# Where the bulk loads are begun, how a step of probabilities is transposed, and four orders of instructions, in a layer of local and global attention with a final linear part

## The chip, the cores and the metric

The kernel runs on one core of a Trainium2 chip. Its time is the device time of one launch in microseconds (us). TensorE (PE) multiplies matrices, VectorE (DVE) and ScalarE (ACT) work on elements, GpSimd (POOL) does casts and begins some transfers, SyncE (SP) begins transfers only. The profile reads one execution of the program.

## The reference

The input is x of shape (4, 1024, 1024): 4 batches, 1024 tokens, 1024 channels, 16 heads of 64. Everything is float32.

```
h  = layernorm(x);  q, k, v = h@Wq+bq, h@Wk+bk, h@Wv+bv        # split into 16 heads of 64
local:  each block of 128 queries attends to 256 keys, [i*128-64, (i+1)*128+64), masked at both ends
idx:    token 0, the 62 tokens of the largest |q| of the head, token 1023
global: softmax(q[idx] k^T / 8) v over all 1024 keys, written over the rows idx of the local result
x = x + ctx
out = x + layernorm(x) @ (w * scale[:, None])^T + bias
```

## The kernel before

A program for each engine is written out by hand. Engines meet at counting semaphores. Every matmul of a projection is done three times: a float32 operand is split into a high part (`_hi`) and the remainder (`_lo`), and hi*hi, hi*lo and lo*hi are added up.

**A batch** has a query part (8 slices of 128 query columns are projected, q is turned, norms are taken, and VectorE begins to find the 62 largest norms, 8 at a time: MAX, FIND_INDEX, MATCH_REPLACE, L1450 to L1454), and then 8 **units**, hp = 0 to 7. A unit is a pair of heads. It has four local steps, s = 0 to 3 (two query blocks of 128 for both heads in each), and a global step, called STEPS in the code. After the four batches come 32 tiles of the final linear part (L799); two of them are done ahead, inside the last unit.

**TensorE in a unit** works in this order: scores 0 (L745), part 0, weigh step 3 of the unit before (L757), part 1, scores 1, global weigh of the unit before (L779), part 2, scores 2, part 3, weigh 0, part 4, scores 3, part 5, weigh 1, part 6, global scores (L771), weigh 2, part 7. A part is 12 of the 96 matmuls (L639) that project the keys and values of the next pair. Parts 0 to 3 make v (two halves of the tokens), 4 to 7 make k. In unit 6 the order is v half 0 (parts 0, 1), k half 0 (2, 3), v half 1 (4, 5), k half 1 (6, 7), and part 6 comes after weigh 2. The halves go through PSUM banks that ScalarE empties: `out("v", 1, 2)` (vT, L1075) empties the bank of v half 1 before k half 1 (part 6) may write there.

**A step of probabilities** takes this way: VectorE takes the row maxima (L1510, L1513); ScalarE takes the exponentials (L1105); VectorE copies them as two planes of 16-bit words, `part_p` (`p_parts<-probs`, L1496); SP begins a transposing DMA, `turn_p` (`p_turned<-p_parts`, L295); ScalarE puts the planes together again, `join_p` (`pT<-p_turned`, L1127); TensorE weighs the values with the result (L757, L779). Each of the copy, the DMA and the join is done in two halves of 1024 words (the last of the global step has 1280). There is one `p_parts` and one `p_turned`. So the DMA of a half waits for the join of the same half of the step before. The values go the same way in three pieces of 768 words (`part_v` L1486, `turn_v` L305, `join_v` L1092).

**SP's order.** All of this program's transfers but the gathers, scatters and the last stores are begun by SP, one behind the other; an instruction of SP that waits for a semaphore holds all behind it. SP begins in each unit, besides the transposing DMAs and the context stores: two loads of 512 KB of the weights' slices (`w_raw`, L387 at the unit's start, L412 in its middle), one of 512 KB with columns of the next batch's x (`load_column`, L322), and in units 0 and 1 two of 512 KB with rows of x (`load_rows`, L314) for the row statistics. POOL splits each slice into its parts (`split`, L500 and L502).

**Row statistics of the next batch** are taken by VectorE (BN_STATS, L1322) in the query part (tile pair 0) and in units 0 to 2 (pairs 1 to 3). `row_roots` follows in unit 3, then SP writes the statistics to DRAM (`save_stats`, L337) at that unit's end and reads them back spread over the partitions (`spread_stats`, L347) at the start of unit 4, ahead of the transposing DMA of step 0. VectorE's normalising of the columns (L1392, L1395) needs them from unit 4 on. In the last batch `spread_scale` and `load_ahead` stand in that place instead, and `load_first` (L372, L373) starts four loads for the final linear part in the last unit.

## Time and profile before

| | before |
|---|---|
| median of 3 runs | 2244.83 us (2239.55 to 2246.85) |
| the profiled execution | 2241.47 us |
| its span | 2239.5 us |
| its mean TensorE clock | 0.95 of full speed |
| TensorE busy | 2039.9 us, 91% |
| units 0 to 6 of the four batches, together | 1237.63 us |

The span is the time from the first to the last instruction of the profile. A unit's length is taken from one unit's first matmul of scores 0 to the next one's.

### The profile page before, as it was taken

How to read it: one execution, taken by the hardware profiler on the slowest of the kernel's cores; microseconds unless marked ns; L12 is line 12 of the kernel's file. 1: busy time of each engine (PE TensorE's matmuls, PEld its weight loads, DVE VectorE, ACT ScalarE, POOL GpSimd, SP SyncE). 2: the span in 40 equal slices, each digit the busy share in tenths (PEclk: the TensorE clock that was granted, in tenths of full speed). 3: DMA queues.
4: the chain of work that ended last, by engine and by line, in shares of the span. 5: the costliest groups of instructions: out<-in, count | busy, mean ns of one | idle time of the engine just before them, and what ended most of it. 6: DMA issues, size and time to landing. Idle time of an engine off the chain costs nothing.

```text
span 2239.5 us, 37450 instructions
## 1 busy us (share of the span) xinstructions
PE 2039.9 (91%) x11264; PEld 1698.9 (76%) x11264; DVE 1524.9 (68%) x2904; ACT 1047.0 (47%) x1979; POOL 523.3 (23%) x336
## 2 busy tenths in 40 slices
PE   6989797999988879999888699998998997999999
PEld 6877685787867767888677578886887876888887
DVE  6687675774876757748777577577785775666664
ACT  4325555683256646742465466624675682000000
POOL 2241121123321121132321312233222202212221
PEclk9999898999989989999999899999999998999999
DMA  4346656654365566643465556524666645333331
GB/s 154 91 103 132 143 123 117 137 121 130 88 146 129 134 114 124 132 130 113 110 135 138 118 132 132 123 83 97 138 142 169 153 78 166 141 131 127 136 140 66
DMA packets 539680, 280.73 MB, mean 125 GB/s; under 512 B 439120, under 2 KB 504726, under 8 KB 539536
## 3 DMA queue, kind: packets, MB, share of 16 engines
q1 hardware_dynamic: 531888, 261.21, 49.0%
q10 hardware_dynamic: 4320, 15.73, 1.7%
q0 software_dynamic: 3328, 2.17, 0.5%
q8 instruction: 54, 0.88, 0.2%
q14 instruction: 90, 0.74, 0.1%
HBM read 122.73 MB, written 51.44 MB: 78 GB/s over the span
## 4 chain that ended last, share of the span: by engine, by line
PE 47%; DVE 18%; DMA 11%; ACT 9%; issue 8%; SPq 6%; DVEq 1%; ACTq 0%; POOL 0%; POOLq 0%
PE proj L639 20%; PE proj L799 15%; DMA p_turned<-p_parts 7%; PE pv L757 4%; ACT pT L1127 4%; SPq L295 3%; DVE x_norm L1454 3%; ACT probs L1105 3%; DVE top_val L1450 2%; DVE p_parts L1496 2%; DVE top_idx L1452 2%; PE score L771 2%; DVE q_sq L1416 2%; DMA stat_rows<-ln_rstd 1%; PE pv L779 1%
## 5 line engine op out<-in xcount | busy, mean ns | idle before, releaser
L639 PE MATMUL proj<-xT_hi,w_hi 128*128 128x512 f32 x1536 | 447.2, 438 | 99.5 <-ACT vT L1075 79.9
L639 PEld LDWEIGHTS proj<-xT_hi,w_hi 128*128 128x128 f32 x1536 | 302.5, 207 | 169.3 <-ACT vT L1075 83.2
L639 PE MATMUL proj<-xT_hi,w_lo 128*128 128x512 f32 x1536 | 425.8, 407 | 0.0
L500 POOL CAST w_hi<-w_raw 128x1024 fp32r<-128x1024 f32 x96 | 114.2, 1189 | 1225.4 <-PE proj L639 1147.6
L639 PE MATMUL proj<-xT_lo,w_hi 128*128 128x512 f32 x1536 | 381.9, 391 | 0.0
L1127 ACT COPY pT<-p_turned 128x1024 uint16<-128x1024 uint16 x256 | 344.0, 1362 | 71.5 <-DMA p_turned<-p_parts 71.5
L639 PEld LDWEIGHTS proj<-xT_hi,w_lo 128*128 128x128 f32 x1536 | 291.6, 196 | 62.9
L639 PEld LDWEIGHTS proj<-xT_lo,w_hi 128*128 128x128 f32 x1536 | 288.5, 188 | 63.7
L1496 DVE COPY p_parts<-probs 128x1024 uint16<-128x1024 uint16 x320 | 259.4, 820 | 113.7 <-ACT probs L1105 58.1
L757 PEld LDWEIGHTS pv<-v_nat,pT 128*128 128x128 f32 x2048 | 261.5, 201 | 78.1 <-issue 68.2
L757 PE MATMUL pv<-v_nat,pT 128*128 128x64 f32 x2048 | 257.2, 281 | 64.8 <-ACT v_nat L1092 64.8
L502 POOL TENSOR_TENSOR w_lo<-w_raw,w_hi 128x1024 fp32r<-128x1024 f32 x96 | 238.7, 2487 | 7.8
L1105 ACT ACTIVATE probs<-turn,neg_max 128x256 f32<-128x256 f32 (+1 forms) x256 | 115.3, 457 | 184.4 <-DVE neg_max L1510 127.0
L1105 ACT ACTIVATE probs<-score,neg_max 128x256 f32<-128x256 f32 (+1 forms) x256 | 116.1, 465 | 95.1 <-DVE neg_max L1513 83.3
L559 POOL TENSOR_TENSOR q_store<-q_store,bias_b 128x1024 f32<-128x1024 f32 x30 | 71.8, 2392 | 332.0 <-DVE q_store L1791 251.8
L1416 DVE TENSOR_TENSOR q_sq<-pT 128x512 f32<-128x512 f32 x64 | 71.8, 1121 | 111.0 <-ACT pT L1049 109.8
L1082 ACT ACTIVATE kT_hi<-proj,bk_c 128x512 fp32r<-128x512 f32 x64 | 44.0, 688 | 181.5 <-PE score L771 143.2
L1519 DVE TENSOR_REDUCE neg_max<-score 128x1 f32<-128x1024 f32 x32 | 39.1, 1223 | 104.3 <-PE score L771 104.3
L1127 ACT COPY pT_g<-p_turned 128x1024 uint16<-128x1024 uint16 x64 | 96.0, 1502 | 15.3 <-DMA p_turned<-p_parts 14.6
L1040 ACT ACTIVATE pT<-proj,bq_c 128x512 f32<-128x512 f32 x48 | 33.1, 689 | 140.8 <-PE proj L639 140.8
L1092 ACT COPY v_nat<-v_turned 128x768 uint16<-128x768 uint16 x96 | 98.4, 1082 | 0.0
L1132 ACT CAST qT_hi<-turn 128x1024 fp32r<-128x1024 f32 x15 | 15.2, 1016 | 159.9 <-PE turn L788 159.9
(169 smaller groups left out, 3068.9 us busy)
## 6 DMA issues: line engine op xcount, KB each, us to landing
w_raw<-in_wstream SPq DMA_DIRECT2D x96, 512.0 KB, 3.8
x_buf<-in_rows SPq DMA_DIRECT2D x55, 512.0 KB, 3.4
q_rows<-pT SPq DMA_DIRECT2D x64, 256.0 KB, 2.4
ctx_rows<-ctx_out SPq DMA_DIRECT2D x128, 128.0 KB, 2.1
q_store<-ctx_rows SPq DMA_DIRECT2D x30, 512.0 KB, 4.1
out<-q_store ACTq DMA_DIRECT2D x30, 512.0 KB, 2.6
q_store<-in_cols SPq DMA_DIRECT2D x28, 512.0 KB, 3.6
p_turned<-p_parts SPq DMA_TRANSPOSE x320, 3.3
```

Source lines behind the costliest of these rows:

```text
L295: sp.dma_start_transpose(p_turned[:, 2 * words.start:2 * words.stop].rearrange("p (x r) -> p x r", r=P), p_parts[:, 2 * words.start:2 * wo ...
L500: pool.tensor_copy(w_hi[b][:, :], w_raw[b][:, :]).then_inc(w_hi_set, 1)
L502: pool.tensor_tensor(w_lo[b][:, :], w_raw[b][:, :], w_hi[b][:, :].bitcast(F32), ALU.subtract).then_inc(w_split[b], 1)
L559: pool.tensor_tensor(lin_hb[:, b, :], lin_h[:, b, :], bias_b[:, :], ALU.add).then_inc(hb_set, 1)
L639: mm = pe.matmul(proj[:, bank, :], w[b][:, k * P:k * P + P], x[:, k, half * HALF:half * HALF + HALF], start=(m == 0), stop=(m == 23), skip ...
L757: mm = pe.matmul(pv[:, g * HD:g * HD + HD], pT_of(s)[:, (g * 2 + c) * P:(g * 2 + c) * P + P], v_nat[:, 2 * s + b + c, h, :], start=(c == 0 ...
L799: mm = pe.matmul(proj[:, half, :], x[b][:, k * P:k * P + P], w[:, k, half * 512:half * 512 + 512], start=(m == 0), stop=(m == 23), skip_gr ...
L1092: act.copy(v_nat[:, 3 * k:3 * k + 3, :, :].rearrange("p t h d -> p (t h d)").bitcast(U16) .rearrange("p (x s) -> p s x", s=2), v_turned[:, ...
L1105: last = act.activation(probs[:, at:at + hi - lo], score_of[s][:, at:at + hi - lo], ACT.Exp, bias=neg_max[:, g:g + 1], accum_out=row_sum[: ...
L1127: act.copy(pT_of(s)[:, words].bitcast(U16).rearrange("p (x s) -> p s x", s=2), p_turned[:, 2 * words.start:2 * words.stop].rearrange("p (s ...
L1416: dve.tensor_tensor(q_sq[:, :], src, src, ALU.mult).then_inc(q_squared[h], 1)
L1496: dve.tensor_copy(p_parts[:, 2 * words.start:2 * words.stop].rearrange("p (s x) -> p s x", s=2), probs[:, words].bitcast(U16).rearrange("p ...
```

## The change

(a) The loads of `w_raw`, of the columns, of row pair 3 and of `load_first` are begun by POOL, each slice's load right after the split that frees a buffer two slices ahead. POOL's loop over units is written out. Row pair 1 is loaded by SP in the query part, row pair 2 between the first and second `turn_v` ahead of unit 0.
(b) Each step has one copy of 2048 words (2304 for the global step), one transposing DMA and one join. Both halves' exponentials come ahead of the join.
(c) On ScalarE `out("v", 1, 2)` comes right after the exponentials of step 2, ahead of the join of step 1, in all units but the last. Before, it came after the joins of step 2.
(d) The row statistics come one unit sooner throughout: pair 1 in the query part, pairs 2 and 3 in units 0 and 1, the roots and `save_stats` in unit 2, `spread_stats` (or `spread_scale`) in unit 3 behind `turn_p` of step 3; `load_ahead` at the end of unit 3.
(e) On VectorE some norm finds come ahead of the copies, `part_v(n, 0, 2)` comes behind the maxima of step 0 in unit 0, the copy of the global step comes ahead of `pv_out(u, 2)`, and the last unit's work for the linear part is put in another order.

```diff
@@ SP
             def turn_p(n, hp, s):
-                i = n * (PAIRS * EVENTS) + hp * EVENTS + s
-                for h in range(2):
-                    words = half_words(s, h)
-                    sp.wait_ge(p_parted, 2 * i + h + 3)
-                    sp.wait_ge(pT_set, 2 * i + h + 1)
-                    sp.dma_start_transpose(...).then_inc(p_moved[h], 16)
+                i, words = n * (PAIRS * EVENTS) + hp * EVENTS + s, words_of(s)
+                sp.wait_ge(p_parted, i + 2)
+                sp.wait_ge(pT_set, i + 1)
+                sp.dma_start_transpose(...).then_inc(p_moved, 16)
...
-            def stores(n, hp, next_slices, following):
+            def stores(n, hp, following):
                 last = hp == PAIRS - 1
-                if next_slices:
-                    sp.wait_ge(w_split[0], n * BUFS + PAIRS // 2 + 3 + hp)
-                    sp.dma_start(w_raw[0][:, :], next_slices[0]).then_inc(raw_in[0], 16)
-                if hp == HALF_PAIRS:
-                    if following:
-                        spread_stats(n)
-                    else:
-                        spread_scale(n)
-                        load_ahead()
                 turn_p(n, hp, 0)
...
-                if hp < 2 and following:
-                    load_rows(n, hp + 2)
-                if hp == 2:
-                    load_last_column(n, following)
-                if last and not following:
-                    load_first()
                 turn_p(n, hp, 2)
...
-                if next_slices:
-                    sp.wait_ge(w_split[1], n * BUFS + PAIRS // 2 + 3 + hp)
-                    sp.dma_start(w_raw[1][:, :], next_slices[1]).then_inc(raw_in[1], 16)
                 turn_p(n, hp, 3)
+                if hp == HALF_PAIRS - 1:
+                    if following:
+                        spread_stats(n)
+                    else:
+                        spread_scale(n)
...
-                if hp == HALF_PAIRS - 1 and following:
+                if hp == HALF_PAIRS - 2 and following:
                     save_stats(n)
+                if hp == HALF_PAIRS - 1 and not following:
+                    load_ahead()
@@ POOL
+            def load_slice(n, i, count):
+                b = i % 2
+                pool.wait_ge(w_split[b], count + 2)
+                pool.dma_start(w_raw[b][:, :], wstream[(i + 2) % SLICES]).then_inc(raw_in[b], 16)
...
@@ ACT
             def attend(...):
...
-                exps(u, 2, 0)
-                before(2, 0)
-                exps(u, 2, 1)
-                before(2, 1)
+                for h in range(2):
+                    exps(u, 2, h)
+                if not last:
+                    out("v", 1, 2)
+                join_p(n, hp, 1)
...
-                before(3, 0)
                 exps(u, 3, 1)
-                before(3, 1)
-                if not last:
-                    out("v", 1, 2)
+                join_p(n, hp, 2)
@@ DVE
+                if hp == 0:
+                    part_v(n, 0, 2)
...
-                if following and hp < HALF_PAIRS - 1:
-                    row_moments(n, hp + 1)
+                if following and hp < HALF_PAIRS - 2:
+                    row_moments(n, hp + 2)
...
+                if following:
+                    row_moments(n, 1)
                 top_rows(n, 0)
...
-                for k in range(1, V_PIECES):
-                    part_v(n, 0, k)
+                part_v(n, 0, 1)
                 k_lo_out(n, 0, 1)
```

SP in unit 0, from the first transposing DMA of step 1 to the second of step 3. Before:

```order
L295 DMA_TRANSPOSE p_turned<-p_parts 128x8x128
L291 REGISTER_ALU
L293 REGISTER_ALU
L295 DMA_TRANSPOSE p_turned<-p_parts 128x8x128
L314 ISA
L314 DMA x_buf<-in_rows 128x1024
L314 ISA
L314 DMA x_buf<-in_rows 128x1024
L291 ISA
L293 REGISTER_ALU
L295 DMA_TRANSPOSE p_turned<-p_parts 128x8x128
```

and the same place of SP's program, now:

```order
L289 DMA_TRANSPOSE p_turned<-p_parts 128x16x128
L285 REGISTER_ALU
L289 DMA_TRANSPOSE p_turned<-p_parts 128x16x128
L279 ISA
L279 DMA ctx_rows<-ctx_out 128x2x128
```

Between the transposes of steps 1 and 2 nothing is left; the two loads of rows with their waits are gone from there, and a step is one DMA of 16 blocks of 128 words.

SP at the border of units 2 and 3, now (`stat_rows` are the statistics in DRAM; the first `p_turned` row is the transpose of unit 3's step 0):

```order
L299 DMA_TRANSPOSE v_turned<-q_sq 128x6x128
L312 REGISTER_ALU
L315 ISA
L315 DMA stat_rows<-ln_mv 128x8x1
L315 ISA
L315 DMA stat_rows<-ln_rstd 128x8x1
L285 REGISTER_ALU
L289 DMA_TRANSPOSE p_turned<-p_parts 128x16x128
L279 ISA
```

The two writes of statistics stood one unit later before, with the loads L322, L387 and L347 between them and the transpose; now the transpose of step 0 is the next transfer.

ScalarE in unit 6, around the join of step 1. Before:

```order
L1127 COPY pT1<-p_turned 128x2x512
L1088 REGISTER_ALU
L1092 COPY v_nat<-v_turned 128x2x384
L1088 REGISTER_ALU
L1092 COPY v_nat<-v_turned 128x2x384
L1100 REGISTER_ALU
L1105 ACTIVATE probs,row_sum<-turn,neg_max 128x256
...
L1127 COPY pT0<-p_turned 128x2x512
L1072 REGISTER_ALU
L1073 REGISTER_ALU
L1075 ACTIVATE vT<-proj,bv_c 128x512
```

and now:

```order
L1108 ACTIVATE probs,row_sum<-score,neg_max 128x256 x2
L1075 REGISTER_ALU
L1076 REGISTER_ALU
L1078 ACTIVATE vT<-proj,bv_c 128x512
L1122 ISA
L1130 COPY pT1<-p_turned 128x2x1024
L1091 REGISTER_ALU
L1095 COPY v_nat<-v_turned 128x2x384
```

The emptying of v half 1 (vT) has moved from behind the last join of step 2 (pT0) to the place ahead of the join of step 1 (pT1).

## Rows read from the trace of the kernel before

**Rows 1.** Waits of TensorE by what ended them: total us, times, longest.
```profile
PE proj L639 <- ACT vT L1075: 79.9, 24, 8.1
PE pv L757 <- ACT v_nat L1092: 64.8, 8, 13.9
```

**Rows 2.** Units 0-6, batch 3, all batches: us; busy by engine; PEclk, DMA share, GB/s.
```profile
1530.96:1816.77 285.81, 268.38 (x1607) 223.19 (x1606) 205.84 (x389) 186.00 (x367) 67.87 (x44) 0.96 0.64 140
sum 1237.63, PE 1087.01 PEld 902.10 DVE 855.53 ACT 740.98 POOL 262.59; mean PE 271.75 PEld 225.52 DVE 213.88 ACT 185.24 POOL 65.65
```

**Rows 3.** Units of batch 1 (0 to 6), then unit 1 of batch 3, same columns.
```profile
611.08:659.02 47.94, 38.87 (x201) 31.63 (x201) 31.67 (x56) 23.41 (x50) 12.96 (x11) 0.86 0.57 124
659.02:706.68 47.66, 39.80 (x234) 32.99 (x233) 31.55 (x59) 26.74 (x53) 7.93 (x4) 0.89 0.62 136
...
752.13:792.87 40.74, 38.91 (x234) 32.34 (x234) 30.86 (x77) 26.87 (x53) 8.40 (x5) 0.96 0.59 132
792.87:850.11 57.24, 41.20 (x234) 34.18 (x234) 33.37 (x58) 26.32 (x53) 13.17 (x12) 0.85 0.63 115
850.11:891.67 41.56, 38.88 (x234) 32.35 (x234) 30.20 (x50) 26.59 (x53) 7.25 (x4) 0.96 0.60 130
891.67:928.76 37.09, 37.09 (x235) 31.13 (x235) 27.00 (x47) 28.32 (x57) 7.37 (x4) 1.00 0.74 146
...
1576.65:1615.02 38.37, 37.28 (x234) 31.20 (x233) 29.80 (x55) 26.66 (x53) 7.97 (x4) 1.00 0.64 141
```

**Rows 4.** Timeline, a stall of unit 1, batch 1.
```profile
684.24 1.51 SPq L314 DMA_DIRECT2D x_buf<-in_rows  x2
686.11 3.92 SPq L295 DMA_TRANSPOSE p_turned<-p_parts  x2
691.36 1.34 ACT L1127 COPY pT<-p_turned 128x1024 uint16<-128x1024 uint16 x1 [4.44 <-DMA p_turned<-p_parts]
695.34 2.08 PE L639 MATMUL proj<-xT_hi,w_hi 128*128 128x512 f32 x4 [7.86 <-ACT vT L1075]
```

**Rows 5.** The transposes of p_parts, and the copy and join beside them.
```profile
DMA to landing us min/median/max: 3.0/3.3/9.2
...
L1127 ACT COPY pT<-p_turned 128x1024 uint16<-128x1024 uint16 x256 | 344.0, 1362 | 71.5 <-DMA p_turned<-p_parts 71.5
L1127 ACT COPY pT_g<-p_turned 128x1280 uint16<-128x1280 uint16 x32 | 52.9, 1654 | 2.3 <-DMA p_turned<-p_parts 2.2
L1496 DVE COPY p_parts<-probs 128x1024 uint16<-128x1024 uint16 x288 | 233.3, 812 | 113.7 <-ACT probs L1105 58.1 <-DMA p_turned<-p_parts 47.9 <-DVE top_val L1450 2.7
```

**Rows 6.** The transposes of v (768 words each), from the tile v_turned.
```profile
DMA to landing us min/median/max: 2.7/2.7/9.5
```

**Rows 7.** The page's DMA issues: KB each, median us to landing.
```profile
x_norm<-stat_rows SPq DMA_DIRECT2D x6, 512.0 KB, 5.9
stat_rows<-ln_rstd SPq DMA_DIRECT2D x3, 4.0 KB, 10.9
```

**Rows 8.** Timeline of unit 6, batch 1, TensorE's global weigh, weigh 0, part 5, weigh 1.
```profile
901.01 2.27 PE L779 MATMUL pv<-v_nat,pT_g 128*128 128x128 f32 x18
909.78 1.89 PE L757 MATMUL pv<-v_nat,pT 128*128 128x64 f32 x16
...
916.38 1.98 PE L639 MATMUL proj<-xT_lo,w_hi 128*128 128x512 f32 x8
918.20 1.89 PE L757 MATMUL pv<-v_nat,pT 128*128 128x64 f32 x16
```

**Rows 9.** Timeline, opening of unit 0, batch 1.
```profile
615.87 1.00 DVE L1486 COPY q_sq<-vT 128x768 uint16<-128x768 uint16 x1 [3.09 <-DMA v_turned<-q_sq]
629.79 1.11 PE L757 MATMUL pv<-v_nat,pT 128*128 128x64 f32 x4 [4.30 <-ACT v_nat L1092]
```

**Rows 10.** Timeline of the last unit of batch 3, at the loads of load_first.
```profile
1850.00 7.81 SPq L295 DMA_TRANSPOSE p_turned<-p_parts  x2
1860.68 1.65 PE L639 MATMUL proj<-xT_hi,w_hi 128*128 128x512 f32 x3 [8.20 <-DVE w_raw L1576]
```

255 lines of the change are left out of this document (128 added, 127 removed).

## The prediction

> **What bounds the kernel now.** I read the waits of TensorE first, then its busy time unit by unit, then the timeline around the largest gaps. TensorE is the engine that sets the end, and where it has no gap a unit takes 37.09 us: unit 6 of batch 1, granted clock 1.00 [rows 3]. The 28 units 0 to 6 take 1237.63 us together [rows 2], so 1237.63 - 28 x 37.09 = 199 us is gaps, and matmuls at half clock behind them. The reader should see in [rows 3] how uneven that is: 47.94, 47.66, 40.74, 57.24, 41.56, 37.09. Two waits hold most of it: for vT, which empties a projection bank (79.9 us, 24 times), and for the turned values at a weighing (64.8 us, 8 times) [rows 1].
>
> Neither ScalarE nor VectorE is late by its own work there. [Rows 4] show a gap of 7.86 us ended by vT: ScalarE had waited 4.44 us for a transposing DMA, because SP stood before the two loads of rows, which wait for VectorE's BN_STATS, and began the two transposes at 686.11 only behind them. A gap also costs afterwards: the 4 matmuls behind it took 2.08 us [rows 4], where 8 of the same shape take 1.98 without a gap [rows 8], so TensorE ran at the lower of its two levels, 1.2 in place of 2.4 GHz. That is 1.1 us on four matmuls, and the granted clock of a unit with a gap (0.86 to 0.89, 1.00 without [rows 3]) says that it lasts longer; I take 1.6 us for each gap of over 2 us.
>
> **The transposing DMA and its ring (b).** One buffer p_turned, so in a unit 5 times: transpose, join, transpose. Half a step (1024 words) lands 3.0 us after its issue at the least and 3.3 at the median [rows 5]; 768 words land after 2.7 [rows 6]. The rows show no DMA of 2048 words. From below it is 3.3 (the added words cost nothing), from above 6.6 (two halves one behind the other). By the slope (3.0 - 2.7) / 256 a word it is 3.0 + 1.2 = 4.2, with rounding 3.8 to 4.7; I take 4.4, and 4.7 for 2304 words. The join: 1362 ns for 1024 and 1654 for 1280 [rows 5], so 1.14 ns a word: 2.53 us for 2048 and 2.82 for 2304. With 0.2 us from one to the other a ring is 4 x (4.4 + 2.53 + 0.2) + (4.7 + 2.82 + 0.2) = 36.2 us, or 5L + 14.2 for a transpose of L. That is just under the 37.09 of TensorE. The joins' busy time falls little (two halves 2.72, one 2.53), the copies likewise (two of 812 ns to one of some 1.2 us, lower bound 0.8, upper 1.6), and it lies beside the join. So (b) gives up the overlap of two halves and gets fewer issues; by itself I give it no gain, only the risk that there is 0.9 us of slack per unit.
>
> Is each use in time? TensorE's places in a clean unit are [rows 8], from 891.67: global weigh at +9.3, weigh 0 at +18.1, weigh 1 at +26.5. Global scores end near +33; k out, maximum, exponential and the join of step 3 bring the global transpose to +38.3, its join ends at +8.9 of the next unit (due 9.3). Step 0: DMA 9.0 to 13.4, join 16.05, the first value piece 17.05 (due 18.1). Step 1: DMA 16.2 to 20.6, join to 23.2, values to 25.2 (due 26.5). These fit by 0.4 to 1.3 us.
>
> **Loads away from SP (a).** Removed from SP's line: two slices, one column load a unit, two loads of rows in units 0 and 1. In [rows 4] the transpose was in after 5.25 us (686.11 to 691.36) against 3.0 at the least [rows 5]: of the 7.86 us some 2.2 are transfer, the rest is SP held. I take the hold as gone in 5 of 7 units. What stays is that 512 KB move beside a transpose now and then. Unit 1 of batch 3, which has no loads of rows, shows what is left: 38.37 us [rows 3]. Its gap is at vT, which (c) frees, but I expect the thin ring to eat as much: 38.3 for an undisturbed unit. POOL's own issue and its waits for the split are covered: it is busy 7.9 us of 47.7 in unit 1 [rows 3], and a slice is asked for most of a unit before it is used.
>
> The Trainium skill ("DMA: Bandwidth & Descriptors", section "Issuing engines are not separate DMA queues") says that beginning transfers on another engine saves only the sequencer's time. By it the transfer part of each collision would stay; that is the second rival. The same page, in "Queues, rings and completion order", says that each DMA engine goes round between queue rows packet by packet; by it a load on POOL's queue shares with a transpose and doesn't stand ahead of it, which is nearer to my 38.3. No row of this trace shows large loads on POOL's queue, so it bears out neither.
>
> **Unit by unit**, batches 0 to 2, before (batch 1) and after:
> - Unit 0, 47.94 to 39.3. On VectorE the wait of 3.09 us for a v transpose stood ahead of the maxima; part_v(2) now stands behind them. That, with 1.0 for the copy itself, covers the wait of 4.30 at weigh 0 [rows 9]. BN_STATS in the query part take 2.4 us away again.
> - Units 1, 2 and 5: 47.66 and 41.56 [rows 3] (unit 2 like unit 1) to 38.3 each.
> - Unit 3, 40.74 to 44.0. The statistics' writes land 10.9 us after their issue [rows 7]. They used to be in unit 4; now they stand right ahead of step 0's transpose in unit 3. Written at about +4, with the transpose wanted at +9: weigh 0 waits 10.9 - 5 - 1.05 = 4.85, and 37.1 + 4.85 + 1.6 + 0.5 (ring) = 44.0.
> - Unit 4, 57.24 to 43.5. Writing, reading back and VectorE's wait fall out; but spread_stats (5.9 us [rows 7]) stands ahead of the global transpose of unit 3. It can cost 0 to 5.5; I take 4.3, and 37.1 + 4.3 + 1.6 + 0.5 = 43.5.
> - Unit 6, 37.09 to 44.5, the loss in (c). There v half 1 is parts 4 and 5, and weigh 1 follows it directly (part 5 ends 918.36, weigh 1 begins 918.20 [rows 8], +26.5). ScalarE now waits for that half, empties it (0.7), and only then joins step 1 (2.5) and a value piece (1.08 or so): +31.0, a gap of 4.5; with 1.6 of clock and 1.3 at weigh 2 behind it: 37.1 + 4.5 + 1.6 + 1.3 = 44.5.
>
> Sum 39.3 + 3 x 38.3 + 44.0 + 43.5 + 44.5 = 286.2, three times 858.6. These batches took 1237.63 - 285.81 = 951.82 [rows 2]: -93.2. Batch 3 has no statistics and no loads of rows: 41.7 (unit 0, where the query part ends sooner and the finds of the indices are later relative to it), 4 x 38.3, 41.5 (unit 4, load_ahead), 44.5: 280.9 against 285.81, -4.9. (e) otherwise changes places of work that VectorE has room for; nothing. In the last unit load_first stood ahead of two transposes, which SP took 7.81 us to get out, and a gap of 8.20 followed [rows 10]: about 6 us back. At the start slices load beside the rows: +2.5 (0 to 5). Sum: -93.2 - 4.9 - 6 + 2.5 = -101.6. The profiled execution took 2241.47, so 2139.9; the median of the runs is 3.4 above that execution: **2143 us**.
>
> **The rivals.**
> 1. *More is gained.* The losses that I see in units 3, 4 and 6 don't come: the statistics' writes run beside the transpose, the spread is done before the global step, or ScalarE's wait is short. 3 x (5.7 + 5.2 + 6.2) + 3.2 + 6.2 = 61 us less: 2082. For it: unit 3 has 10 us before weigh 0. Against: rows show small writes that take 10.9, and unit 6's order is plain in the program.
> 2. *Loads are in the way as before, or the ring binds.* A transpose takes 5.2 instead of 4.4: 5 x 5.2 + 14.2 = 40.2 a unit, some 2.1 more in 28 units: 2143 + 59 = 2202. For it: the median transpose of half a step is 0.3 above the least already, and the longest 9.2.
> 3. *Slower.* The same ring, further on. Transposes can't overlap each other any more, so every transfer that meets one delays the whole ring and each unit after it. The point: a mean unit of (1237.63 + 3.5) / 28 = 44.3, which is L = 6.0. At 6.5 a unit is 46.7, 28 x 46.7 = 1308, +71 - 3.5: 2312. For it: L = 6.6 is the upper bound above, and up to five loads of 512 KB fall in a unit. Against: the slope of [rows 5, 6].
> 4. *No change.* SP's hold was only a cover, and L comes out at 6.0: 2245.
>
> **How the numbers follow.** Forecast 0.50, with 2110 to 2175 as its own range; rival 1 0.25; rival 2 0.12; rival 3 0.09; rival 4 0.04. The range 2070 to 2215 leaves out the tail of rival 1 (0.05), a little of rival 2 (0.02) and rivals 3 and 4 (0.13). A difference under 0.3% (6.7 us) can't be told from none. Faster: 0.50 + 0.25 + 0.12 = 0.87; same 0.04; slower 0.09.
>
> **What would show it.** Right: waits of TensorE for vT under 20 us; transposes of p_parts landing at 4.2 to 4.7; units 1, 2 and 5 at 37.1 to 38.5; in unit 6 of every batch a gap of 3 to 6 us ahead of weigh 1 with ScalarE's vT just before it; in unit 3 a gap at weigh 0 with the statistics ahead of the transpose. Wrong: a median landing over 5 us, or units 1, 2 and 5 over 40; POOL's loads landing so late that TensorE waits for a split; or unit 6 still at 37.

## The result and the profile after

The changed kernel takes 2270.64 us (median of 8 runs, 2255.98 to 2278.9) against 2245.84 us (8 runs, 2239.55 to 2250.28): a ratio of 1.0111, 95% interval 1.0084 to 1.0137. It is 1.1% slower. The prediction was 2143 us, 4.6% faster, with a range up to 2215. The profiled execution took 2275.79 us, its span 2274.2.

TensorE's waits after the change, by what ended them (us in total, times, longest), against [rows 1]:

```profile
PE pv L782 <- ACT pT_g L1130: 67.7, 23, 8.0
PE pv L760 <- ACT v_nat L1095: 49.0, 12, 8.2
PE pv L760 <- DVE ctx_out L1526: 32.0, 18, 2.2
PE score L675 <- DVE q_store L1350: 18.9, 1, 18.9
PE proj L642 <- DVE kT_lo L1431: 9.3, 4, 2.9
```

All 79.9 us of waits for vT are gone. In their place stand 67.7 us for the join of the global step (pT_g), of which before had 4.7, and 32.0 us for ctx_out, of which before had none. Unit by unit, batch 1 (against [rows 3]), then units 0 to 6 of batch 3 and of all batches (against [rows 2]); us, busy time of each engine, granted clock:

```profile
627.94:668.96 41.02, 36.42 (x201) 29.64 (x201) 30.55 (x49) 22.77 (x46) 14.59 (x13) 0.92 0.64 145
668.96:715.38 46.42, 40.62 (x234) 33.67 (x233) 34.28 (x53) 27.03 (x48) 10.27 (x8) 0.93 0.60 128
715.38:753.98 38.60, 37.44 (x234) 31.05 (x233) 29.81 (x61) 26.04 (x48) 10.11 (x7) 1.00 0.65 140
753.98:801.60 47.62, 42.07 (x234) 34.73 (x233) 31.47 (x64) 27.07 (x48) 9.64 (x8) 0.89 0.73 117
801.60:845.04 43.44, 39.04 (x236) 32.14 (x235) 28.00 (x45) 25.70 (x48) 17.07 (x15) 0.96 0.66 144
845.04:890.34 45.30, 39.06 (x235) 32.69 (x235) 31.18 (x45) 27.32 (x48) 10.02 (x7) 0.96 0.55 122
890.34:950.11 59.77, 46.42 (x234) 38.35 (x234) 32.38 (x51) 32.17 (x56) 8.85 (x7) 0.80 0.48 96
...
1554.13:1869.77 315.64, 283.62 (x1607) 235.39 (x1606) 208.50 (x355) 188.74 (x337) 79.54 (x65) 0.91 0.60 128
sum 1278.42, PE 1123.13 PEld 931.34 DVE 864.14 ACT 753.00 POOL 318.94; mean PE 280.78 PEld 232.84 DVE 216.04 ACT 188.25 POOL 79.73
```

Units 0 to 6 take 1278.4 us in place of 1237.6: +40.8. Of the gaps of over 0.45 us in them I counted 36 with 150.6 us before and 52 with 154.5 us after. So the idle time hardly changed, and TensorE's busy time grew by 36.1 us (1123.1 - 1087.0) with the same matmuls. The granted clock says why: in these units TensorE was busy for 119 us at the lower of its two levels before and for 188 us after. A matmul takes twice as long there ([rows 4] against [rows 8]), so half of the 69 us more, 34.5, is lost to it: nearly all of the 36.1. The rest of the difference of the spans (34.7 us): the first unit begins 8.5 us later (154.89 against 146.44), unit 7 and the query parts take 3.8 more, and the stretch from the last unit 7 to the end takes 18.3 less (404.4 against 422.7).

Batch 3 lost most: 315.64 against 285.81. It had no loads of rows, and so little to win from their removal.

The local transposes and the joins themselves are what the prediction said. The landing of p_turned's DMA (issue to landing, min/median/max), two tile lines and the copy's line of the page:

```profile
DMA to landing us min/median/max: 4.2/4.4/11.2
...
L1130 ACT COPY pT<-p_turned x128: 2453/2535/2568, 174.0 to 1907.7; 128x2048 uint16<-128x2048 uint16 x128
L1130 ACT COPY pT_g<-p_turned x32: 2757/2788/2842, 207.1 to 1917.8; 128x2304 uint16<-128x2304 uint16 x32
...
L1491 DVE COPY p_parts<-probs 128x2048 uint16<-128x2048 uint16 (+1 forms) x160 | 246.5, 1540 | 232.8 <-DMA p_turned<-p_parts 197.1
```

4.4 us (4.4 forecast), 2.53 us (2.53) and 2.79 us (2.82). The 4.4 is the median of all steps; the global step's transposes are another matter, see below. VectorE's copy took 1.23 us at the median (1.2 forecast) and 1.54 at the mean, since 26 of the 160 took 2 to 3.6 us; all 26 were due while an instruction of POOL's split ran. VectorE now waits 197.1 us for the DMA of the step before, in 76 of 160 steps, where it waited 47.9 [rows 5], in 26 of 320 half steps. The ring is tight in half of the steps.

The border of units 5 and 6 in batch 1, timeline (start, us, engine, line, idle before and what ended it):

```profile
890.65 1.38 DVE L1482 COPY q_sq<-vT 128x768 uint16<-128x768 uint16 x1 [1.78 <-DMA v_turned<-q_sq]
891.70 2.58 POOL L453 TENSOR_TENSOR w_lo<-w_raw,w_hi 128x1024 fp32r<-128x1024 f32 x1
891.95 3.55 DVE L1491 COPY p_parts<-probs 128x2304 uint16<-128x2304 uint16 x1
894.88 0.75 POOL L461 DMA_DIRECT2D w_raw<-in_wstream  x1 [0.59 <-POOL w_lo L453]
895.42 0.41 DVE L1526 TENSOR_TENSOR ctx_out<-pv,row_inv 128x256 f32<-128x256 f32 x1
895.67 6.35 SPq L289 DMA_TRANSPOSE p_turned<-p_parts  x1
895.73 0.53 POOL L477 DMA_DIRECT2D q_store<-in_cols  x1
896.07 1.99 PE L760 MATMUL pv<-v_nat,pT 128*128 128x64 f32 x16 [1.79 <-DVE ctx_out L1526]
904.38 2.77 ACT L1130 COPY pT_g<-p_turned 128x2304 uint16<-128x2304 uint16 x1 [5.29 <-DMA p_turned<-p_parts]
907.21 2.08 PE L782 MATMUL pv<-v_nat,pT_g 128*128 128x128 f32 x8 [5.41 <-ACT pT_g L1130]
```

Everything that the change put near this border meets here. VectorE waits for a transpose of v and copies v's third piece; the global copy then runs beside POOL's split and takes 3.55 us; ctx_out, which now stands behind that copy, lets TensorE wait 1.79 us. POOL begins two loads of 512 KB 0.8 us ahead of and 0.06 us behind the global transpose, which holds SP for 6.35 us and comes in 8.7 us after its issue. TensorE then waits 5.41 us for the join. Over the whole trace I sorted the 32 global transposes by the bulk loads that POOL began from 1.5 us ahead of them to 2.1 us behind. With none (16 times) they landed after 4.53 to 5.82 us, 4.57 at the median; with one (4 times) after 6.46 to 6.98; with two (12 times) after 7.24 to 11.24, 7.85 at the median. The four with one load all end unit 3, where SP's own `spread_stats` or `spread_scale` stands right ahead of them too.

Unit 6 of the same batch, ahead of weigh 1:

```profile
927.09 0.69 ACT L1078 ACTIVATE vT<-proj,bv_c 128x512 f32<-128x512 f32 x1 [8.82 <-PE proj L642]
927.67 2.48 ACT L1130 COPY pT<-p_turned 128x2048 uint16<-128x2048 uint16 x1
...
930.02 1.94 ACT L1095 COPY v_nat<-v_turned 128x768 uint16<-128x768 uint16 x2
931.18 3.67 PE L760 MATMUL pv<-v_nat,pT 128*128 128x64 f32 x16 [4.29 <-ACT v_nat L1095]
```

ScalarE idles 8.82 us for the second half of v, and only then empties it and joins step 1. The gap is 4.29 us; [rows 8] have none there, and the forecast was 4.5.

### The profile page after: what moved, and what is told of

Its sections match the earlier page's. It is cut to its first block, busy times and chain, and to the rows that moved or that the text cites. A ratio compares the mean times of both kernels' runs of the same rounds, so it can differ in the third digit from the quotient of the medians.

```text
span 2274.2 us, 35808 instructions
## 1 busy us (share of the span) xinstructions
PE 2072.1 (91%) x11264; PEld 1723.4 (76%) x11264; DVE 1521.3 (67%) x2744; ACT 1046.5 (46%) x1819; POOL 606.9 (27%) x474
## 3 DMA queue, kind: packets, MB, share of 16 engines
q1 hardware_dynamic: 506896, 188.83, 38.3%
## 4 chain that ended last, share of the span: by engine, by line
PE 44%; DMA 20%; DVE 16%; ACT 9%; issue 7%; SPq 3%; DVEq 1%; ACTq 0%
PE proj L642 17%; DMA p_turned<-p_parts 16%; PE proj L802 14%; ACT pT L1130 4%; PE pv L760 4%; DVE p_parts L1491 4%; DMA v_turned<-q_sq 3%; ACT pT_g L1130 3%; PE pv L782 2%; DVE top_val L1446 2%; DVE x_norm L1450 2%; DVE top_idx L1448 2%; SPq L289 2%; DVE q_sq L1412 1%; PE turn L791 1%
## 5 line engine op out<-in xcount | busy, mean ns | idle before, releaser
L642 PE MATMUL proj<-xT_hi,w_hi 128*128 128x512 f32 x1536 | 427.5, 423 | 10.2 <-DVE kT_lo L1431 9.3
L1491 DVE COPY p_parts<-probs 128x2048 uint16<-128x2048 uint16 (+1 forms) x160 | 246.5, 1540 | 232.8 <-DMA p_turned<-p_parts 197.1
L451 POOL CAST w_hi<-w_raw 128x1024 fp32r<-128x1024 f32 x96 | 104.3, 1086 | 1075.6 <-PE proj L642 821.3
L1130 ACT COPY pT<-p_turned 128x2048 uint16<-128x2048 uint16 x128 | 324.0, 2531 | 104.7 <-DMA p_turned<-p_parts 102.4
L760 PE MATMUL pv<-v_nat,pT 128*128 128x64 f32 x2048 | 273.0, 292 | 90.8 <-ACT v_nat L1095 49.0
L642 PEld LDWEIGHTS proj<-xT_hi,w_hi 128*128 128x128 f32 x1536 | 292.9, 201 | 72.9 <-DVE kT_lo L1431 10.2
L782 PE MATMUL pv<-v_nat,pT_g 128*128 128x128 f32 x576 | 95.2, 336 | 67.7 <-ACT pT_g L1130 67.7
L782 PEld LDWEIGHTS pv<-v_nat,pT_g 128*128 128x128 f32 x576 | 88.8, 244 | 73.6 <-ACT pT_g L1130 72.6
L1482 DVE COPY q_sq<-vT 128x768 uint16<-128x768 uint16 x96 | 73.4, 765 | 91.9 <-DMA v_turned<-q_sq 60.3
L1130 ACT COPY pT_g<-p_turned 128x2304 uint16<-128x2304 uint16 x32 | 89.4, 2793 | 89.0 <-DMA p_turned<-p_parts 88.9
```

The lines of the kernel that those rows point to most:

```text
L451: pool.tensor_copy(w_hi[b][:, :], w_raw[b][:, :]).then_inc(w_hi_set, 1)
L642: mm = pe.matmul(proj[:, bank, :], w[b][:, k * P:k * P + P], x[:, k, half * HALF:half * HALF + HALF], start=(m == 0), stop=(m == 23), skip ...
L760: mm = pe.matmul(pv[:, g * HD:g * HD + HD], pT_of(s)[:, (g * 2 + c) * P:(g * 2 + c) * P + P], v_nat[:, 2 * s + b + c, h, :], start=(c == 0 ...
L782: mm = pe.matmul(pv[:, 0:P], pT_g[:, j * P:j * P + P], v_nat[:, j, :, :].rearrange("p h d -> p (h d)"), start=(j == 0), stop=(j == TILES))
L1130: act.copy(pT_of(s)[:, 0:words].bitcast(U16).rearrange("p (x s) -> p s x", s=2), p_turned[:, 0:2 * words].rearrange("p (s x) -> p s x", s= ...
L1482: dve.tensor_copy(v_parts[:, :, :], vT[:, 3 * P * k:3 * P * k + 3 * P].bitcast(U16) .rearrange("p (x s) -> p s x", s=2)).then_inc(v_parted, 1)
```

## The experiments

In all of them each transposing DMA is replaced by a plain DMA of as many bytes, from SBUF to SBUF, in rows of 256 bytes (in the source each row begins 64 bytes behind the one before, so that the rows overlap). Probabilities and values don't reach their places; everything else is computed. No variant with transposing DMAs was run, so that what follows is shown for this stand-in, and for the changed kernel only as far as the two agree:

```diff
-                sp.dma_start_transpose(p_turned[...].rearrange("p (x r) -> p x r", r=P), p_parts[...])
+                sp.dma_start(p_turned[...].rearrange("p (x r) -> p x r", r=P), rows_of(p_parts[...]))
```

The names begin with p_ for that; s_before_h is the kernel before with this edit alone, and p_after the changed kernel. A ratio is to the kernel before with its transposing DMAs, run on the same chip between the others; its median lay between 2242.8 and 2251.0 us, so I compare ratios first.

**How near the stand-in is (s_before_h, p_after).**

> The kernel before, in which each transposing DMA is a plain DMA of the same bytes, from SBUF to SBUF in rows of 256 bytes; the transposition is left out, so probabilities and values are not in their places. It is one half of a pair that asks whether the loss of 1.1% stays when nothing transposes. If a plain row costs as much as a transposing one, a half step lands 3.0 us after its issue and the time is 2240 to 2250; if plain rows are faster, landings near 2.0 to 2.5 and a time of 2170 to 2230.

Measured: 2238.5 us in one run, against 2244.1 of the kernel before beside it. Halves land at 3.0 us (3.3 with transposition), the waits for vT are 74.2 us in 24 gaps (79.9 in 24). For the kernel before, the stand-in is good to 0.3%.

> The changed kernel with each transposing DMA replaced by a plain DMA of the same bytes in rows of 256 bytes (the transposition is left out, so probabilities and values are not in their places). The kernel before with the same plain DMAs took 2238.5 us. Theory A (the loss is made by order and by loads beside the global step's DMA, not by the transposition as such): same waits as in the changed kernel, for ctx_out about 1.8 us in each of some 18 units, for the global join in over 15, in unit 6 one of over 3 us ahead of weigh 1; the time is 2245 to 2280. Rival (a transposing DMA is what suffers beside loads): the global step's DMA lands within 5 us beside two loads, the waits for the global join fall under 20 us, and the time is under 2200.

Measured: 2195.57 us, ratio 0.976 (0.9735 to 0.9786). The rival was right on the time, and the changed kernel is 2.4% faster with plain DMAs, 1.1% slower with transposing ones. Its waits are of the same kinds, only fewer:

```profile
PE pv L766 <- ACT v_nat L1101: 51.9, 12, 7.4
PE pv L788 <- ACT pT_g L1136: 34.7, 18, 5.0
...
PE pv L766 <- DVE ctx_out L1532: 14.8, 9, 2.1
```

From the issue to a join that waited for it, a local step's plain DMA took 4.20 us at the median without a POOL load near it (4.39 transposing). With a load begun 0.6 to 1.2 us ahead it took 5.6 to 6.6 us (7 times), the transposing one 5.5 to 6.7 (6 times). With two loads begun near the global one it took 7.9 to 8.3 us (3 times), the transposing one 7.3 to 11.4, 7.9 at the median (12 times). So a plain DMA suffers nearly as well from a load begun just ahead of it; what differs most is how often they meet: two loads stand beside 3 of 32 global steps here and beside 12 of 32 with transposing DMAs. The border of units 5 and 6 again, in this kernel:

```profile
852.30 1.36 DVE L1497 COPY p_parts<-probs 128x2304 uint16<-128x2304 uint16 x1
...
854.04 0.59 SPq L295 DMA_DIRECT2D p_turned<-p_parts  x1
854.64 2.37 POOL L459 TENSOR_TENSOR w_lo<-w_raw,w_hi 128x1024 fp32r<-128x1024 f32 x1
...
857.60 0.56 POOL L467 DMA_DIRECT2D w_raw<-in_wstream  x1 [0.59 <-POOL w_lo L459]
...
862.68 1.49 PE L788 MATMUL pv<-v_nat,pT_g 128*128 128x128 f32 x11 [1.22 <-ACT pT_g L1136]
```

Here the copy is in time: it is over (1.36 us) before the split's subtraction starts, the DMA has 3.6 us before the loads, and the gap is 1.22 in place of 5.41. The price is on POOL's side: its cast, the first half of the split, began in the same moment as the copy and took 2.25 us, not some 1.03.

**Undoing (b): halves again (p_halves).** One edit on p_after: copy, DMA and join are loops over two halves, at the same places.

```diff
+                for h in range(2):
+                    words = half_words(s, h)
+                    sp.wait_ge(p_parted, 2 * i + h + 3)
+                    sp.wait_ge(pT_set, 2 * i + h + 1)
+                    sp.dma_start(...).then_inc(p_moved[h], 16)
```

> The changed kernel with plain DMAs (p_after) and part (b) undone: each copy, DMA and join is done in two halves again, at the same places of the program. Theory K (one DMA per step gave up the overlap of a DMA with the join of the other half, and this made the ring tight): with halves the ring has slack again, waits for the global join fall from 34.7 us to under 10 and the time to 2160 to 2180. Rival (the number of issues and semaphores counts): the time rises, to over 2205.

Measured: 2125.6 us, ratio 0.946 (0.9444 to 0.9476); 70 us less than with single pieces, more than expected. Waits for the global join 11.3 us in 5. Batch 1, units 1 to 6:

```profile
635.90:673.20 37.30, 37.30 (x235) 31.03 (x235) 32.13 (x60) 26.92 (x53) 10.04 (x8) 1.00 0.65 160
673.20:710.32 37.12, 37.12 (x234) 31.11 (x233) 31.39 (x66) 26.74 (x53) 9.22 (x7) 1.00 0.59 145
710.32:752.26 41.94, 39.04 (x235) 32.65 (x235) 30.45 (x68) 26.53 (x53) 9.85 (x8) 0.96 0.79 149
752.26:793.42 41.16, 38.97 (x234) 32.35 (x233) 32.55 (x52) 25.61 (x52) 15.43 (x15) 0.96 0.60 139
793.42:830.55 37.13, 37.13 (x234) 31.10 (x234) 31.32 (x53) 27.90 (x54) 10.06 (x7) 1.00 0.59 145
830.55:875.40 44.85, 40.51 (x234) 33.92 (x233) 28.06 (x54) 30.85 (x61) 8.46 (x7) 0.92 0.53 129
```

Units 1, 2 and 5 are at TensorE's floor. Unit 6 is 44.3 to 45.3 us in the four batches (44.5 forecast), with 4.2 to 4.3 us of gap ahead of weigh 1 as the prediction had it. The rest of what is left stands in unit 3 (45.3, 41.9 and 44.4 in batches 0 to 2, 44.0 forecast), unit 4 (43.7, 41.2 and 40.2, forecast 43.5) and unit 0 (45.4, 42.8 and 42.8, forecast 39.3).

**(b) alone, on the kernel before (p_before_single).** The same edit the other way round: one copy, DMA and join, at the place of the second half.

> With plain DMAs (the transposition is left out): the kernel before (2238.5 us so) with part (b) alone: one copy, one DMA and one join per step, each at the place of the second half. Theory (the single pieces make the ring longer by what the halves overlapped): in the changed kernel (b) cost 70 us; here the ring is behind the loads of SP too, so that it costs as much or more: 2290 to 2350. Rival (the kernel before has gaps of its own that would cover it): 2235 to 2270.

Measured: 2275.23 us, ratio 1.0127 (1.0107 to 1.0147). +37 us on the 2238.5 of the stand-in, between the two ranges: the direction was right, the size under the theory's. That the gaps which the kernel before has anyway cover a part of it is the likely reading; it was not tried.

**How steep the ring is (p_rows17, p_rows18).** Each local step's DMA is made one or two rows of 256 bytes per partition longer.

```diff
+                if s < STEPS:
+                    words += 1 * P // 2      # 2 * P // 2 in p_rows18
```

> The changed kernel with plain DMAs (p_after, 2195.6 us; the transposition is left out), each of the four local steps' DMAs made one row of 256 bytes per partition longer (17 in place of 16; the words added are used by nothing). From the joins that waited, the plain DMA is in after 4.20 us and the transposing one after 4.39: 0.2 us. One row more should add some 0.16 us, so four of them 0.6 us to a unit's ring. Theory K (knife edge: the ring has no slack left, and once it is late, the global copy falls beside POOL's split and its DMA beside POOL's two loads, which keeps it late): the time jumps to 2235 to 2275, near the changed kernel's, with over 15 waits for ctx_out. Rival L (linear): at most 28 x 0.64 = 18 us more, 2196 to 2214. Rival T (a transposing DMA is what suffers beside a load, 6.26 us against 4.85 beside one load): nothing changes, 2190 to 2205.

> As p_rows17 with two rows more (18 in place of 16), some 0.32 us for each local step, 1.3 us for a unit. Theory K: 2260 to 2300, at or over the changed kernel's 2270. Rival L: at most 36 us more, 2196 to 2232. Rival T: under 2215.

Measured: 2218.98 us (0.9876, 0.9859 to 0.9892) and 2243.5 us (0.9979, 0.9955 to 1.0002); the second spread from 2226 to 2246 in 9 of 10 runs. Issue to join 4.36 and 4.50 us against 4.20. So 0.16 us on 4 of 5 DMAs of a unit, 0.64 us a unit and 18 us for 28, cost 23, and twice that 48: no jump (theory K fell), but over the upper bounds of theory L too (2214 and 2232). Every 0.1 us of the DMA comes through, and somewhat more: the slack that the prediction counted isn't there.

**SP's issue (p_slow_issue, p_rows17_slow).** A transposing DMA of a step keeps SP 1.9 us at the median, a plain one 0.6. Twenty increments behind the plain one make it 1.8.

```diff
+                for _ in range(20):
+                    sp.sem_inc(idle, 1)
```

> With plain DMAs (the transposition is left out): the changed kernel (p_after, 2195.6 us) with 20 increments of an idle semaphore on SP behind each DMA of a step, to make SP's issue as long as that of a transposing DMA (1.9 us at the median against 0.6). Theory I (SP's longer issue holds the context stores and the transfers of v behind it, and this makes a part of the 75 us between plain and transposing DMAs): 2210 to 2240. Rival (SP has room for it): within 6 us of 2195.6.

> With plain DMAs (the transposition is left out): the changed kernel with one row of 256 bytes more in each local step's DMA and with the 20 increments on SP behind it, so that landing alone (some 4.36 us against 4.39) and SP's hold are near those of the transposing DMAs. If the two add up (23.4 and 16.6 us alone): 2236, and of the 75 us between plain and transposing DMAs some 35 stay for what a transposing DMA loses beside loads (6.26 us against 4.85 beside one load). If they amplify each other (knife edge): over 2255. If one covers the other: under 2225.

Measured: 2212.17 us (0.9836, 0.9807 to 0.9865) and 2212.7 us (0.9872, 0.9827 to 0.9918). The first gives 17 us to a hold of 1.8 us. The two don't add up: one covers the other. Together they are 1.1 points of the 3.5 between 0.976 and 1.0111. The imitation is even, and the real hold is not: 36 of the 160 transposes of the changed kernel hold SP for over 3 us, up to 6.8, and the longest of them stand beside POOL's loads. No run imitates that.

**Where the slices are loaded (p_sp_slices, p_halves_sp_slices).** The two weight slices of a unit, and those of the query part, go back to SP at their old places; columns, row pair 3 and the first loads of the linear part stay on POOL.

```diff
+                if next_slices:
+                    sp.wait_ge(w_split[0], n * BUFS + PAIRS // 2 + 3 + hp)
+                    sp.dma_start(w_raw[0][:, :], next_slices[0]).then_inc(raw_in[0], 16)
                 turn_p(n, hp, 0)
```

> With plain DMAs (the transposition is left out): the changed kernel with single pieces (p_after, 2195.6 us), and the slices loaded by SP again at their old places. Theory (with single pieces the global step's DMA meets POOL's loads at the border of two units; on SP they stand behind or ahead of it and never beside it): the waits for the global join fall from 34.7 us to under 20 and the time by 10 to 30 us. Rival (SP is held by the waits for the split, which single pieces with their tight ring can't bear): 2200 to 2230.

> With plain DMAs (the transposition is left out): the changed kernel with its halves back (p_halves, 2125.6 us), and the slices of the weights loaded by SP again at their old places; rows and columns stay where the change put them. Theory (SP's waits for POOL's split held the DMAs behind them): 25 to 60 us of the gain go, 2150 to 2185, with gaps ended by vT again. Rival (the rows' and columns' loads held SP, not the slices'): 2120 to 2140.

Measured: with single pieces 2157.58 us (0.9594, 0.9565 to 0.9623), 38 us less than p_after; with halves 2120.51 us (0.9419, 0.9384 to 0.9455), not to be told from p_halves. With single pieces the waits for the global join fall from 34.7 to 17.9:

```profile
PE pv L780 <- ACT v_nat L1115: 54.9, 12, 7.3
PE pv L802 <- ACT pT_g L1150: 17.9, 14, 2.3
```

So beginning the slices on POOL brings nothing with halves, and costs 38 us with single pieces. With halves, SP's waits for the split cost nothing that shows. The Trainium skill ("DMA: Bandwidth & Descriptors", section "Issuing engines are not separate DMA queues") says that another issuing engine saves only the sequencer's time; by p_halves against p_halves_sp_slices the runs agree. With single pieces the loads also changed their place among the transfers, from behind or ahead of the global step's DMA to beside it, and there 38 us hang on it.

**(c) for itself (p_halves_vt_late, p_before_vt_early).** out("v", 1, 2) is moved and nothing else. In p_before_vt_early unit 6 (`early`) keeps its old order, and the move is ahead of the second half of step 1's join.

```diff
@@ p_before_vt_early, on the kernel before
                 exps(u, 2, 1)
+                if not last and not early:
+                    out("v", 1, 2)
                 before(2, 1)
...
-                if not last:
+                if early:
                     out("v", 1, 2)
```

> With plain DMAs (the transposition is left out): the changed kernel with its halves back (p_halves, 2125.6 us) and (c) undone in all units: out(v, 1, 2) behind the joins of step 2. Theory C (the gain of the changed order lies in (c), since putting the slices back on SP cost nothing): the gaps ended by vT come back in units 0 to 5, 1.3 us at the least in each of 24, less the gaps in unit 6: 2140 to 2180. Rival D (the gain lies in the loads and waits for rows that are gone from SP between step 1 and step 2, part (d)): 2110 to 2130.

> With plain DMAs (the transposition is left out): the kernel before (2238.5 us so) with (c) alone: out(v, 1, 2) right behind the exponentials of step 2, in all units but 6 and 7. Theory C: the 74.2 us of gaps ended by vT go in units 0 to 5 with their clock (24 x 1.6); what is late then is step 1's weighing in units 1 and 2, by the time SP is held, so that perhaps half comes: 2160 to 2200. Rival D (the join of step 1 is as late as vT in the units with loads of rows, and the gap moves to weigh 1): 2205 to 2240.

Measured: undone in the changed order with halves, 2179.61 us (0.9683, 0.9651 to 0.9716), 54 us more, with 47.0 us of waits for vT in 24 gaps. Alone on the kernel before, 2162.27 us (0.961, 0.9582 to 0.9637): 76 us less than s_before_h. Nothing of its 74.2 us of waits for vT is left:

```profile
PE pv L763 <- ACT v_nat L1098: 72.8, 8, 17.1
PE pv L785 <- ACT pT_g L1133: 18.4, 10, 2.2
```

This one line moved on ScalarE is the largest single gain that was measured: 76 us in the order before, 54 in the changed one. It is not all. The rest of the change, with halves, is worth 59 us without it (2238.5 against 2179.6) and 37 with it (2162.3 against 2125.6). The slices have no part in that; the loads of columns and rows off SP, (d) and (e) were not told apart.

**The smaller losses (p_ctx_first, p_vt_late_unit6, p_loads_behind_g, p_stats, p_halves_ctx_vt).**

```diff
@@ p_ctx_first, DVE
+                pv_out(u, 2)
                 if not last:
                     part_v(n, hp + 1, 2)
                 part_p(n, hp, STEPS)
-                pv_out(u, 2)
@@ p_vt_late_unit6, ACT
-                if not last:
+                if not last and not early:
                     out("v", 1, 2)
...
                 join_p(n, hp, 2)
+                if early:
+                    out("v", 1, 2)
@@ p_loads_behind_g, POOL, ahead of the slice load at a unit's start
+                    pool.wait_ge(p_moved, behind)      # the global step's DMA has landed
@@ p_stats, SP
-                    sp.dma_start(stat_rows[n, i].rearrange("(t p) -> p t", p=P), src, ...
+                    sp.dma_start(stat_rows[n, i].rearrange("(p t) -> p t", p=P), src, ...
```

> The changed kernel with plain DMAs (the transposition is left out) and one more edit: on VectorE pv_out(u, 2) stands again ahead of the third copy of v and the copy of the global step. Theory A (the border of two units is decided by the chain global copy, global DMA, global join; the wait for ctx_out lies in its shadow): TensorE's 18 waits for ctx_out (32 us) go, and its waits for the global join grow by nearly as much; the time moves by -20 to +5 us from that of the changed kernel with plain DMAs. Rival B (the two gaps add up, each with its lower clock): 32 + 18 x 1.6 = 61 us less.

Measured: 2185.44 us, 0.971 (0.9688 to 0.9732). 10 us less. The waits for ctx_out fell by 13 us and those for the global join rose from 34.7 to 48.0: the wait lay in the shadow of the chain behind it, as theory A has it.

> The changed kernel with plain DMAs (the transposition is left out) and one more edit: in unit 6 alone out(v, 1, 2) stands again behind the join of step 2. Theory A (in unit 6 ScalarE waits for the second half of v before it may join step 1, and weigh 1 follows that half directly): the gaps of 4.3 us ahead of weigh 1 and those ahead of weigh 2 (1.9 to 3.1) go in all batches: 4 x (4.3 + 2.0 + 1.6 to 3) = 32 to 37 us less than the changed kernel with plain DMAs. Rival B (the ring was late there already and the wait only names the last one): a gap of over 2 us stays and the time falls by under 10 us.

Measured: 2176.82 us, 0.967 (0.9645 to 0.9695), 19 us less. Unit 6 fell from 46.6, 49.6, 50.7 and 45.2 us to 40.6, 39.1, 40.9 and 38.3, 33 us in all, and its gaps ahead of weigh 1 are gone. But unit 7 and the query part behind it took 12 us more; in unit 7 TensorE now waits for the casts of the columns (1.9 us each for xT_hi and xT_lo in batches 0 and 2), which come later. The mechanism is shown; a third of it is given back.

> The changed kernel with plain DMAs (the transposition is left out) and one more edit: POOL's slice load at each unit's start, and the column load behind it, wait until the DMA of the global step has landed. Theory A (loads on POOL's queue take their share of the DMA engines from the one transfer that is due next; with two loads it lands after 7.7 us, alone after 4.6): median landing of the global step's DMA about 4.6, TensorE's wait for the global join from 66 us to under 20, time 35 to 60 us less than the changed kernel with plain DMAs; the wait for ctx_out stays. Rival B (the global DMA is late because its copy is late, behind v's third copy and beside the split): landings fall, yet the gap moves to step 0 or stays, and the time falls by under 15 us. Rival C: loads held back make the split late, and TensorE waits for w_lo.

Measured: 2192.1 us, 0.9751 (0.9724 to 0.9778): nothing. The waits for the global join halve (34.7 to 18.3), the global DMA reaches its join after 4.5 us, and the waits at v_nat rise from 51.9 to 61.6: the loads then meet local steps (18 of those that a join waited for have two loads begun from 3 us ahead of the DMA to the join, and take 5.5 us at the median). Theory A fell here: the loads cost wherever they meet a transfer of a tight ring.

> The changed kernel with plain DMAs (p_after), and the row statistics written to DRAM in the order in which they lie in SBUF, 32 bytes in one piece per partition in place of 8 pieces of 4 bytes (so the statistics come back in the wrong order). Theory (the small writes hold the DMA engines for some 10 us, and in unit 3 the global step of unit 2 and step 0 stand behind them): unit 3 of batches 0 to 2 falls from 50 to 52 us to 38 to 41 and the time by 30 to 40 us, to 2156 to 2166. Rival (the wait is for VectorE's roots, which end late in unit 2): unit 3 stays over 46 and the time falls by under 12 us.

Measured: 2172.29 us, 0.9662 (0.9646 to 0.9678), 23 us less: between the two. Unit 3 of batches 0 to 2 went from 52.5, 50.4 and 49.6 to 46.5, 45.8 and 50.8 us, 9 us in all, so the larger part of the 23 came elsewhere. The small writes are a part of unit 3's loss; what else is late there was not taken apart.

> With plain DMAs (the transposition is left out): the changed kernel with its halves back (p_halves, 2125.6 us), pv_out(u, 2) ahead of the copies again, and in unit 6 out(v, 1, 2) behind the join of step 2 again. Theory: what these two cost is apart from what (b) costs. The gap of 4.3 us ahead of weigh 1 in each unit 6 goes (17.2 us and 4 x 1.8 of clock, less what comes late in unit 7), and ctx_out's last waits (5.9 us in unit 4): 2095 to 2108. Rival: with halves they are covered, and the time stays within 8 us of 2125.

Measured: 2120.61 us, 0.9423 (0.94 to 0.9445), 5 us under p_halves (0.4 points by the ratios). The rival was right: with halves both are nearly covered, and ctx_out's wait is still there, 5.9 us in three units 6.

**The parts that pay, together (p_best).** Halves, slices on SP, ctx_out first, vT late in unit 6; of the change it keeps (c), (d) and the other loads on POOL.

> With plain DMAs (the transposition is left out): the changed kernel with halves, slices on SP, pv_out(u, 2) ahead of the copies and, in unit 6, out(v, 1, 2) behind the join of step 2. It keeps of the change (c) outside unit 6, (d) and the rows', columns' and first loads on POOL. If the parts add up: 2120.5 (slices and halves) less 5 to 25: 2095 to 2116. If they don't: 2117 to 2125.

Measured: 2110.01 us (2098.6 to 2111.42), 0.9362 (0.9327 to 0.9396). It is the fastest of all, in the stand-in, though its interval overlaps that of p_halves_sp_slices (0.9384 to 0.9455): a kernel in this order with transposing DMAs was not run. The transposition costs the kernel before 0.3%, and it may cost this one more.

## Why the prediction was wrong

**The step that failed** is the one on (b): "by itself I give it no gain, only the risk that there is 0.9 us of slack per unit", and "these fit by 0.4 to 1.3 us". The sum 5L + 14.2 was right in its local terms and its joins (4.4, 2.53, 2.79), and 36.2 is under 37.09. Its global transpose was forecast at 4.7 us; it took 4.57 in half of the units and 6.5 to 11.2 in the other half. And the sum is the length of a ring in which nobody is late. The trace of after shows who is: VectorE's copies stand behind v's copies, which wait for v's transposes in the same queue (60.3 us in 31 waits), the global copy took up to 3.55 us beside the split, joins stand behind exponentials. Each of these was some tenths to two us, and the ring had 0.9 for all of them. Measured in the stand-in, (b), which was given no gain and no cost, costs 70 us in the changed order and 37 in the order before. My reading is that the halves had been a buffer: one half's DMA went on while the other was joined.

How much of the miss this is: with halves the stand-in takes 2125.6 us, under the forecast of 2143; with single pieces 2195.6, inside the range; and the changed kernel with transposing DMAs 2270.6. So (b) is 70 us, and 75 more come only with transposing DMAs; of these the landing and SP's even hold are 1.1 points, some 25 us, and the rest is open. That 2125.6 lies so near the forecast is partly luck, since the gain came from another place than the prediction had it.

**(a) was mis-ascribed.** The prediction took nearly all of its 93 us in batches 0 to 2 from SP's being freed of loads. The slices' part of it is nothing with halves, and with single pieces they cost 38 us on POOL. The gaps at vT were in the main due to ScalarE's order: vT waited behind two joins. The prediction had that edit in its hand ("which (c) frees") and gave its gain to the thin ring instead. (c) alone, outside unit 6, is worth 76 us on the kernel before. That the gap of [rows 4] began with SP held was true, and the hold counted: without (c), the rest of the change took the waits for vT from 74.2 to 47.0 us, still in 24 gaps. That the hold had to reach TensorE was not true: with vT out of the line these waits are gone and SP's order is as it was.

**Unit by unit.** For units 1, 2 and 5 I forecast 38.3. They are 37.1 to 37.7 with halves, 37.1 to 38.9 with plain single DMAs but for one of 47.0, and with transposing ones anything from 37.1 to 50.2. Unit 4: 43.5 forecast; 44.9, 43.4 and 43.0 in batches 0 to 2. Unit 6: the gap ahead of weigh 1 was right in place, cause and size (4.5, 4.29; 17.1 us in four batches), but the unit took 53.4, 59.8, 59.1 and 48.0, not 44.5. In batch 1 ctx_out, the global join and weigh 2 let TensorE wait 9.1 us more, and the clock was 0.80. Unit 3: 44.0 forecast; 48.3, 47.6 and 42.3 in batches 0 to 2, and 49.1 in batch 3, which has no statistics.

**The collision.** I gave a load beside a transpose some 2.2 us of transfer and let them meet "now and then". They meet at 16 of 32 global steps, because POOL's load begins when the split ends, at the unit's start, just when the global transpose is due. In the order before, SP issued those loads behind the global transposes by its own program order. One load near it, with SP's own spread of the statistics, costs the global transpose 1.9 to 2.4 us (6.46 to 6.98 against 4.57), two cost 3.3 at the median. So the price of one meeting was right; what the prediction had wrong is how often they meet, what two together cost, and that there was no room for it.

**The tail and the start.** load_first off SP: the gap of 8.20 [rows 10] is 0.8 now, and the stretch to the end is 18.3 us shorter, three times the 6 I gave; how much of that is (e)'s new order in the last unit was not told apart. The start is 8.5 us later, over the upper bound of 5. TensorE's first work waits 18.9 us in place of 15.1, as the slices load beside the rows: with the slices on SP (p_sp_slices) it waits 14.9 again, and unit 0 begins 4.3 us sooner than in p_after (150.5 against 154.8).

**The rivals.** Rival 2 (the ring binds, or loads are in the way) was the mechanism, at a chance of 0.12, and its 2202 is near the 2195.6 of the stand-in; it is 69 us short of the changed kernel. (Its 40.2 a unit is 1.9 over the forecast's 38.3, not 2.1, which makes it 2196.) Rival 3 came out on the right side for nearly the right reason, but not by its price: L is 4.4, far under its point of 6.0. What made the mean unit 45.7 us (1278.4 / 28), over the 44.3 of no change, was lateness added to L, not L.

**What stays open.** Plain against transposing: 0.3% in the kernel before, 3.5 points in the changed one. The landing alone (+0.2 us) and SP's even hold (1.8 against 0.6) make 1.1 points together. The rest goes with the number of meetings: two loads stand beside 3 global steps in p_after (profiled at 2194.7 us), 5 in p_slow_issue (2211.8), 6 in p_rows17_slow (2213.3) and p_rows17 (2219.2), 8 in p_rows18 (2225.7) and 12 in the changed kernel (2275.8). Whether the meetings make the kernel late or a late kernel makes the meetings, these traces can't say. Two candidates for what brings them about were not tried by themselves: SP's hold of up to 6.8 us beside loads, and a load begun right behind the DMA. With one begun 0.9 us behind, three transposing DMAs of a local step took 6.6 to 7.1 us to the join and the only plain one 4.2.

## What to carry to other kernels

A ring that just fits, by the sum of its medians, was late here: count each engine's queue at the places where a step changes hands, and compare the slack with the single delays. Here it was 0.9 us, and one copy held by the split (2.2 us more) or one load beside a DMA (2 us more) was already over it. Pieces that overlap in a chain of copy, DMA and join were worth more here (37 and 70 us) than the issues that they cost. When a wait ends at ScalarE, look first for what stands ahead of that instruction on ScalarE and could stand behind it; that was one line here, worth 54 to 76 us, where moving 96 slice loads to another engine was worth nothing with halves and cost 38 us with single pieces.

## What the runs showed of the hardware

- VectorE's copy of 2304 16-bit words took 3.55 us beside POOL's subtraction (2.58 us) and 1.36 right ahead of it. The Trainium skill ("SBUF — State Buffer", section "Who interferes with whom") says that a VectorE instruction in a two-port mode, which a copy can enter, and a GpSimd instruction exclude each other for a whole instruction, whichever began first. The trace agrees, if the copy ran in such a mode: 2.3 us were left of POOL's instruction when the copy was due, and 1.2 to 1.4 is its own time. The other way round, POOL's cast took 2.25 us beside the copy and some 1.03 alone.
- A plain DMA of 512 KB from SBUF to SBUF in rows of 256 bytes lands almost as a transposing one does: 4.20 against 4.39 us to the join. It keeps SP 0.6 us, at most 0.61 in p_after; the transposing one keeps SP 1.9 us at the median and up to 6.8.
- With two loads of 512 KB from POOL's queue begun near it, either kind took about 8 us to the join at the median. With one begun 0.6 to 1.2 us ahead, the plain one took 5.6 to 6.6 and the transposing one 5.5 to 6.7.
- The number of gaps counts, not only their sum: 36 gaps with 150.6 us and 52 gaps with 154.5 us differ by 36 us of busy time of the same matmuls, since TensorE was busy for 188 us at the lower level in place of 119. In batch 1 the granted clock was 0.80 to 0.96 in the units with gaps of over 1.7 us and 1.00 in unit 2, whose only gap was about 1.1 us.
